# Four graph layers on one core: the softmax division moved behind the value products, leaky relu moved into a ScalarE pass, and the hardware loop written out

## The reference

```python
# layer 0: 8 heads of 16
scores = einsum('bhid,bhjd->bhij', q, k) / sqrt(16) + adj[:, None] * W_e
attn   = softmax(where(adj != 0, scores, -inf), axis=-1)
out    = einsum('bhij,bhjd->bhid', attn, v)      # heads joined, then @ W_o.T
# layer 3: 4 heads of 32
e    = leaky_relu(e_i[..., :, None] + e_j[..., None, :], 0.2)
attn = softmax(where(adj > 0, e, -9e15), axis=-1)
out  = einsum('bhnm,bhmd->bhnd', attn, h)        # heads joined
```

## Time and profile before

| | |
|---|---|
| Median of three timed runs | 2156.44 us (2151.73 to 2159.11) |
| Span of the profiled execution | 2151.3 us; its own time outside the span isn't recorded |
| TensorE matmuls busy | 1993.5 us, 93% of the span |
| VectorE busy | 1669.4 us, 78% |
| ScalarE busy | 1344.1 us, 62% |
| GpSimd busy | 733.6 us, 34% |
| Mean granted TensorE clock | 0.986 of full speed |

### The profile page before, as it was taken

The page is one execution under the profiler, slowest core; times in us unless marked ns, Lnnn a source line. Parts: engine busy times, 40 slices in busy tenths (PEclk is TensorE's granted clock), DMA queues, the critical chain, the costliest instruction groups (busy, mean ns, idle before and its releaser), DMA issues. The chain is left out here.

```text
span 2151.3 us, 43160 instructions
## 1 busy us (share of the span) xinstructions
PE 1993.5 (93%) x13642; PEld 1550.2 (72%) x13642; DVE 1669.4 (78%) x4088; ACT 1344.1 (62%) x4769; POOL 733.6 (34%) x925
## 2 busy tenths in 40 slices
PE   5999999999999999999999999999999999999965
PEld 4777877777777777776777877777776777877643
DVE  4577888878878788787888878778787887888764
ACT  3556667666657667566666656666566666667645
POOL 2233343332343233343333343223343333343220
PEclk9999999999999999999999999999999999999986
DMA  2000000000000000000000000000000000000000
GB/s 84 16 21 21 26 26 21 26 21 12 26 27 21 22 11 26 27 26 22 21 11 26 26 27 21 22 11 26 27 26 22 21 11 27 26 26 6 11 6 10
DMA packets 24296, 47.68 MB, mean 22 GB/s; under 512 B 3283, under 2 KB 3284, under 8 KB 23892
## 3 DMA queue, kind: packets, MB, share of 16 engines
q1 hardware_dynamic: 24020, 44.33, 6.4%
HBM read 35.93 MB, written 8.39 MB: 21 GB/s over the span
## 5 line engine op out<-in xcount | busy, mean ns | idle before, releaser
L759 ACT ACTIVATE e<-sc,nm 128x128 f32<-128x128 f32 x1024 | 399.9, 409 | 65.0 <-DVE nm L995 64.9
L766 ACT ACTIVATE pT<-T 128x512 f32<-128x512 f32 x256 | 158.0, 617 | 299.9 <-PE T L462 299.7
L510 PE MATMUL O<-pT,vpad 128*32 128x128 f32 x2048 | 271.6, 276 | 20.7 <-ACT pT L766 20.7
L992 DVE SCALAR_TENSOR_TENSOR sc<-an,rowb,S 128x512 f32<-128x512 f32 x256 | 189.7, 741 | 124.6 <-PE S L490 78.0
L490 PEld LDWEIGHTS S<-kh,qT 128*128 128x128 f32 x2048 | 268.9, 191 | 9.4
L510 PEld LDWEIGHTS O<-pT,vpad 128*32 128x32 f32 x2048 | 202.9, 109 | 99.3 <-issue 47.2
L490 PE MATMUL S<-kh,qT 128*128 128x128 f32 x2048 | 269.9, 275 | 0.0
L421 POOL TENSOR_SCALAR zplus<-tz 128x512 f32<-128x512 f32 x32 | 28.6, 895 | 596.7 <-issue 571.1
L1003 DVE TENSOR_TENSOR p<-e,rec 128x512 f32<-128x512 f32 x256 | 210.4, 822 | 8.8
L759 ACT ACTIVATION_READ_ACCUMULATOR e<-sc,nm 128x1 f32 x1024 | 213.6, 209 | 0.0
L844 ACT ACTIVATE e<-l,nm 128x128 f32<-128x128 f32 x512 | 201.4, 421 | 7.8 <-DVE nm L1139 7.8
(11 more groups left out here) (191 smaller groups left out, 4465.0 us busy)
## 6 DMA issues: line engine op xcount, KB each, us to landing
xt<-in_x_t SPq DMA_DIRECT2D x32, 256.0 KB, 2.7
an<-in_adj_n SPq DMA_DIRECT2D x32, 256.0 KB, 3.1
xn<-in_x_n SPq DMA_DIRECT2D x32, 256.0 KB, 3.7
at<-in_adj_t SPq DMA_DIRECT2D x32, 256.0 KB, 2.7
out_x<-xo SPq DMA_DIRECT2D x32, 256.0 KB, 2.1
wm<-in_mats SPq DMA_DIRECT2D x1, 1472.0 KB, 6.4
wm<-in_mats SPq DMA_DIRECT2D x1, 832.0 KB, 4.5
att<-in_att SPq DMA_DIRECT2D x8, 0.1 KB
```

Source lines behind the costliest of these rows:

```text
L510: last = mm(O[r, b * N:(b + 1) * N], vpad[:, c:c + 32], g(pT0[:, h % 2, :], b), start=(h % 2 == 0 and b == 0), stop=(h % 2 == 1), skip_gro ...
L759: last = fn(g(e0[:, h % 2, :], b), g(sc0[:, h % 2, :], b), ACT.Exp, bias=nm0[:, h % 2, b:b + 1], accum_out=sum0[:, h % 2, b:b + 1])
L766: fn(pT0[:, h % 2, :], T[:, :], ACT.Copy).then_inc(q["pT_ready"], 1)
L992: v.scalar_tensor_tensor(out=sc0[:, h % 2, :], in0=an[p][:, :], scalar=we[:, h:h + 1], in1=S[h % 2][:, :], op0=ALU.mult, op1=ALU.add).then ...
```

## The change

There are three edits.

1. **The division moves.** TensorE now transposes the undivided exponentials `e0` and `e3`. The sums of all heads are kept. In layer 0, VectorE takes one reciprocal of 128x32 sums (`norm`, slot 8), GpSimd spreads it to 128x512 (`spread_sums`), TensorE transposes that into `T` (`sums_T`, slot 11, four transpositions), ScalarE copies it to `recT` (slot 11, in place of the copy of `O`), and VectorE's `out_heads` (slot 10) multiplies `O` by `recT` into `oT`. `project_out` comes after this. In layer 3, `layer3_end` takes one reciprocal of 128x16 sums and multiplies the transposed result by it, ahead of the addition of `x3`.
2. **Leaky relu moves.** ScalarE's pass that adds e_i uses the function Prelu with slope 0.2 and writes `l3` directly. VectorE's max pass and `z3` are gone.
3. **The loop is written out.** All 36 steps are straight code on every engine, and so are the DMA queue's.

```diff
 def steps(eng, step):
-    for t in range(6):
-        step(t // 2, t % 2, phases_of(t))
-    with eng.Fori(3, GROUPS // 2 - 1) as k:
-        step(k, 0, [True] * 6)
-        step(k, 1, [True] * 6)
-    for t in range(GROUPS - 2, GROUPS + 4):
+    for t in range(GROUPS + 4):
         step(t // 2, t % 2, phases_of(t))
...
-            with sp.Fori(2, GROUPS // 2 - 1) as k:
+            for k in range(2, GROUPS // 2 - 1):
...
+            def spread_sums(s):                      # GpSimd, after zx of the step
+                pool.wait_ge(q["rec_done"], s + 1)
+                wait(pool, q["recT_ps"], s)
+                pool.tensor_copy(recx[:, :, :, :], rec0[:, :, :].unsqueeze(3).broadcast_to([128, GB, H0, D0]))\
+                    .then_inc(q["recx_done"], 1)
...
 def probs_T(s, h):                                    # TensorE
-    pe.wait_ge(q["p_ready"], 8 * s + h + 1)
+    pe.wait_ge(q["exp_done"], 8 * s + h + 1)
...
-    transpose4(T, p0[:, h % 2, :]).then_inc(q["tr_ps"], 1)
+    transpose4(T, e0[:, h % 2, :]).then_inc(q["tr_ps"], 1)
...
+            def sums_T(s):
+                pe.wait_ge(q["recx_done"], s + 1)
+                pe.wait_ge(q["pT_ready"], 8 * s + 8)
+                for b in range(GB):
+                    last = nc.tensor.transpose(g(T, b), recx[:, b, :, :].rearrange("p h d -> p (h d)"), ident[:, :])
+                last.then_inc(q["recT_ps"], 1)
...
                     if l0 and i == H0 + 3:
+                        sums_T(t)
                         project_out(t)
...
-                            act.wait_ge(q["pv_ps"], 8 * t + 8)
-                            wait(act, q["wo_ps"], t)
-                            fn(oT[:, :], O[:, :], ACT.Copy).then_inc(q["oT_ready"], 1)
+                            act.wait_ge(q["recT_ps"], t + 1)
+                            wait(act, q["oT_ready"], t)
+                            fn(recT[:, :], T[:, :], ACT.Copy).then_inc(q["recT_ready"], 1)
...
 # ScalarE, layer 3: the exponential of head h, and the bias pass of head h
-                    wait(act, q["p3_ready"], H3 * u + h - 1)
+                    wait(act, q["tr3_ps"], H3 * u + h - 1)
...
-                    wait(act, q["l3_done"], H3 * u + h - 1)
+                    wait(act, q["exp3_done"], H3 * u + h - 1)
                     for b in range(GB):
-                        last = fn(g(z3[:, h % 2, :], b), g(L[:, h % 2, :], b), ACT.Identity,
-                                  bias=h3[:, b, N + h:N + h + 1])
-                    last.then_inc(q["z3_ready"], 1)
+                        last = fn(g(l3[:, h % 2, :], b), g(L[:, h % 2, :], b), ACT.Prelu,
+                                  bias=h3[:, b, N + h:N + h + 1], alpha=SLOPE)
+                    last.then_inc(q["l3_done"], 1)
...
+            def norm(s):                             # VectorE, slot 8
+                dve.wait_ge(q["exp_done"], 8 * s + 8)
+                wait(dve, q["recx_done"], s)
+                v.reciprocal(rec0[:, :, :], sum0[:, :, :]).then_inc(q["rec_done"], 1)
+
+            def out_heads(s):                        # VectorE, slot 10, ahead of masks(t + 1)
+                dve.wait_ge(q["recT_ready"], s + 1)
+                dve.wait_ge(q["pv_ps"], 8 * s + 8)
+                wait(dve, q["wo_ps"], s)
+                v.tensor_tensor(oT[:, :], O[:, :], recT[:, :], ALU.mult).then_inc(q["oT_ready"], 1)
...
 def layer3_end(u, p, k):
+                dve.wait_ge(q["exp3_done"], H3 * u + H3)
+                v.reciprocal(rec3[:, :, :], sum3[p][:, :, :]).then_inc(q["rec3_done"], 1)
+                dve.wait_ge(q["rec3_done"], u + 1)
                 dve.wait_ge(q["o3n_ps"], u + 1)
...
+                v.tensor_tensor(r3[:, :].rearrange("p (c d) -> p c d", d=D3),
+                                L[:, 0, :].rearrange("p (c d) -> p c d", d=D3),
+                                rec3[:, :, :].rearrange("p b h -> p (b h)").unsqueeze(2)
+                                .broadcast_to([128, GB * H3, D3]), ALU.mult).then_inc(q["n3_done"], 1)
+                dve.wait_ge(q["n3_done"], u + 1)
                 dve.wait_ge(ln_out[2], u + 1)
-                v.tensor_tensor(r3[:, :], L[:, 0, :], x3[p][:, :], ALU.add).then_inc(q["r3_done"], 1)
+                v.tensor_tensor(r3[:, :], r3[:, :], x3[p][:, :], ALU.add).then_inc(q["r3_done"], 1)
```

More of the change, by code:

```diff
@@ L113, in build @@
         e0 = sb("e0", [128, 2, W])
-        sum0 = sb("sum0", [128, 2, GB])
-        rec0 = sb("rec0", [128, 2, GB])
-        p0 = sb("p0", [128, 2, W])
+        sum0 = sb("sum0", [128, GB, H0])
+        rec0 = sb("rec0", [128, GB, H0])
+        recx = sb("recx", [128, GB, H0, D0])
+        recT = sb("recT", [128, W])
         pT0 = sb("pT0", [128, 2, W])
@@ L167, in build @@
         e3 = sb("e3", [128, 2, W])
-        sum3 = sb("sum3", [128, 2, GB])
-        rec3 = sb("rec3", [128, 2, GB])
-        p3 = sb("p3", [128, 2, W])
+        sum3 = [sb(f"sum3{p}", [128, GB, H3]) for p in range(2)]
+        rec3 = sb("rec3", [128, GB, H3])
         pT3 = sb("pT3", [128, 2, W])
@@ L424, in step @@
                     pool.tensor_tensor(zx[:, :], zplus[:, :], x1T[:, :], ALU.mult).then_inc(q["zx_done"], 1)
+                if l0:
+                    spread_sums(t)
                 if ahead:
@@ L613, in layer2 @@
                     pe.wait_ge(q["x2T_ready"], u + 1)
-                    wait(pe, q["r3_done"], u - 1)
+                    wait(pe, q["n3_done"], u - 1)
                     for b in range(GB):
@@ L756, in exps @@
                 act.wait_ge(q["nm_ready"], 8 * s + h + 1)
-                wait(act, q["p_ready"], 8 * s + h - 1)
+                wait(act, q["tr_ps"], 8 * s + h - 1)
+                if h == 0:
+                    wait(act, q["rec_done"], s)
                 for b in range(GB):
                     last = fn(g(e0[:, h % 2, :], b), g(sc0[:, h % 2, :], b), ACT.Exp, bias=nm0[:, h % 2, b:b + 1],
-                              accum_out=sum0[:, h % 2, b:b + 1])
+                              accum_out=sum0[:, b, h:h + 1])
                 last.then_inc(q["exp_done"], 1)
@@ L841, in layer3 @@
                     act.wait_ge(q["nm3_ready"], H3 * u + h + 1)
-                    wait(act, q["p3_ready"], H3 * u + h - 1)
+                    wait(act, q["tr3_ps"], H3 * u + h - 1)
+                    if h == 0:
+                        wait(act, q["rec3_done"], u - 1)
                     for b in range(GB):
                         last = fn(g(e3[:, h % 2, :], b), g(l3[:, h % 2, :], b), ACT.Exp,
-                                  bias=nm3[:, h % 2, b:b + 1], accum_out=sum3[:, h % 2, b:b + 1])
+                                  bias=nm3[:, h % 2, b:b + 1], accum_out=sum3[p][:, b, h:h + 1])
                     last.then_inc(q["exp3_done"], 1)
@@ L1121, in layer3 @@
             def layer3(u, i):
[L1122 to L1129, removed]
                 if 5 <= i < 5 + H3:
                     h = i - 5
[L1133 to L1137, removed]
                     dve.wait_ge(q["l3_done"], H3 * u + h + 1)
@@ L1165, in step @@
                         layer2(t - 2, i, p)
-                    if l0 and i in (H0 - 1, H0):
-                        norm(t, i - 1)
                     if l3:
                         layer3(t - 3, i)
-                    if l0 and 0 <= i - 1 < H0 - 2:
-                        norm(t, i - 1)
+                    if l0 and i == H0:
+                        norm(t)
+                    if l0 and i == H0 + 2:
+                        out_heads(t)
                     if l1 and i == 4:
```

34 lines of the change are left out of this document (13 added, 21 removed).

## The result

The changed kernel takes 2251.05 us (median of four runs, 2248.93 to 2251.21) against 2155.53 us for the kernel before: 1.044 times as long, 95% interval 1.0422 to 1.0457, 95.5 us slower. The prediction had the sign and most of the mechanism, but put the time at 2195 us and the end of its range at 2219, so the measured time lies outside.

A forecast was written before the change was run, and what follows sets the result against it. TensorE, in order and filling 61.12 of 62.62 us, was taken as the bound. Span 2151.3 - 49.6 + 66 + 25 + 2 + 0 - 4 gave 2190.7, hence 2195 us measured; range 2163 to 2219.

The forecast's parts named there:

- The jumps: Loop written out: eleven jumps back and their VectorE issue waits go, 4.5 us each, -49.6 us.
- The join: Slot 11: project_out waits behind sums_T, recT and out_heads while TensorE idles; about 2.05 us a step, +66 us.
- GpSimd's spreading: GpSimd's spreading of layer 0's reciprocals ends well ahead of sums_T, so it costs nothing.
- Prelu: ScalarE's bias pass with Prelu costs the same 385 ns as before, so 0; upper end +16 us.
- The gap ahead of `ll`: VectorE finishes ll late, so TensorE waits 0.9 us ahead of the product using it, in 28 steps, +25 us.
- TensorE's transposition of `yT` just doesn't wait: Behind out_heads, yT ends 1.63 us after project_out's start; TensorE transposes it at 1.98 us, without waiting.
- The tail: Steps 32 to 35: max pass and a product go, a multiplication comes; 1.3 us for each of three groups, -4 us.
- only the join shows: Rival: VectorE's lateness is absorbed because ll has more slack than read; 2168 us, chance 0.17.
- faster: Rival: TensorE's two old gaps, at 454.20 and 470.00, disappear as ScalarE gets inputs earlier; 2137 us, chance 0.07.

The follow-up runs named there:

- straight code: The kernel before with its loop written out and nothing else changed; 2105.45 us, ratio 0.9768 to the kernel before.
- Prelu alone: Kernel before, loop written out, two ScalarE copies moved to VectorE, both divisions as before, Prelu replacing VectorE's max pass; 2058.27 us, ratio 0.9550 to the kernel before.
- the two copies: Head 4's transposed exponentials and layer 3's head 1 copied by VectorE instead of ScalarE; on the kernel before with its loop written out, 2068.95 us.
- layer 3's part: Kernel before with loop written out, plus layer 3's division behind its value products and Prelu, layer 0 as before; 2132.19 us.
- the early transpositions of the sums: Changed kernel with sums_T and ScalarE's copy of it moved to slot 10, ahead of layer 3's head 2; 2125.59 us.
- three passes before `ll`: Kernel before with loop written out, plus three unused VectorE reductions ahead of msg; 2169.46 us, ratio 1.0066 to the kernel before.
- two passes before `ll`: Kernel before with loop written out, plus two unused VectorE reductions ahead of msg; 2126.26 us, ratio 0.9864 to the kernel before.

## Why the prediction was wrong

The prediction's sum starts from the span of 2151.3 us; the span after is 2247.2.

- **The jumps**, -49.6 us: right, 48.9 measured alone.
- **The join**, 2.05 us a step: right, 2.01 measured (the prediction's own terms add up to 2.02).
- **GpSimd's spreading** at nothing: right; it took 0.61 us and TensorE never waited for it.
- **Prelu** at the price of the old pass, without a table load: right, these rows of the changed kernel stand against the earlier trace rows:

```profile
L867 ACT ACTIVATE l<-L,h 128x128 f32<-128x128 f32 x512 | 142.0, 376 | 96.0 <-issue 76.6 <-PE L L665 16.5
...
L750 ACT ACT_TABLE_LOAD x1 | 1.3, 1283 | 23.3 <-PE S L471 23.3
```

- **The gap ahead of `ll`**, 0.9 us: right in its place and in what makes it, 1.02 us as idle time and 1.09 us a step as time. Its size is near by luck. Counted from project_out, `ll` starts 1.82 us later than in straight code, not 1.1: front_end 1.14 us late instead of 0.58, and `xo` took 2.84 us instead of 2.48. But TensorE itself is 0.50 us late there, and the slack of 0.29 us was read rightly.
- **"TensorE's transposition of `yT` just doesn't wait"**: wrong. It waits 0.23 us, and from start to start this place costs 0.50 us a step, some 13 us in the full steps, for which the sum had nothing. `yT` was priced at 0.69 us and took 1.41, beside GpSimd's `kh`. In straight code `yT` runs ahead of project_out and `kh` 1.4 us after its start; now `yT` stands behind the join, and `kh` starts 0.3 us after it, because ScalarE copies the keys while TensorE waits. By the Trainium skill, "GPSIMD Engine Reference", section "1. Specifications", GpSimd shares its SBUF interfaces with VectorE, and VectorE instructions with two SBUF inputs contend; the row agrees.
- **The tail**, -4 us: wrong; from the last front_end to the end it is 126.2 us after and 125.7 before. Prelu alone, on straight code with the two copies, gives 3.5 us there. With layer 3's part alone the tail is 126.7 us against 125.9 in straight code, so its division seems to give Prelu's gain back; by which wait wasn't examined.
- **The step that failed** is the one that turned gaps into time, "a new gap of 0.9 us ... +25 us": it counted a gap at its length and took TensorE's clock as full. No term of the sum held the half clock, and neither did an end of the range. The runs show 18 steps longer by 1.62 us, 29 of the 56 us that the forecast missed, with 18 fewer when the gap goes and 15 new ones when such a gap is made by itself. The rows had a warning: the step with a jump has a clock of 0.97, and its own gap ahead of `ll` is the 1.04 us shown above. The late `yT` is another 13 us of the miss, the `ll` term at 1.10 instead of 0.9 us a step 5, and the tail 4.

In numbers, from straight code alone (span 2104.4) to the changed kernel (2247.2) it is 142.8 us: 27 steps at 3.61 us are 97.5 (the prediction had 2.95, or 80); the half clock in them is 29; up to the fourth front_end it is 12.4 (10 forecast, the clock falls in three of these steps too); the last step ahead of the tail is 2.6; single longer steps are 0.8; the tail is +0.3.

The rival "only the join shows" was wrong about the slack, "faster" about ScalarE: the two old gaps are 0.56 and 0.91 us after, as before. Moving work from ScalarE closed them, and the early transpositions of the sums filled part of the second (0.33 us left).

## What to carry to other kernels

An engine that is busy 97% of each step and takes its work in order gained nothing here from another engine's relief; look for what stands directly ahead of its gaps. A chain across three engines in the middle of its list cost its whole latency where it stood, and almost nothing one slot earlier, where other work was at hand. And price a gap of TensorE of about a microsecond at more than its length, at the least as the upper end: here a wait of 1.0 us cost 1.1, plus 1.6 in two steps of three.

## What the runs showed of the hardware

- TensorE's clock went to 1.2 GHz behind a gap ahead of the product with `ll`, by the length of the gap in full steps: 1.22 to 1.58 us, 15 of 27 (three passes before `ll`); 1.01 to 1.35 us, 18 of 27 (changed kernel); 1.04 to 1.06 us, 3 of 11 (kernel before, steps with a jump); 0.88, 1.01 and 1.02 us, all three (layer 3's part). With 0.80 and 0.88 us in two steps (two passes before `ll`), and with 0.76 us or less in the full steps of every kernel, it never did.
- The half clock began 0.8 to 2.3 us after the gap's end and lasted 3.4 us in all these steps. A gap of 1.41 us in the join, by itself, brought none in full steps. Steps of one kernel with the same work and the same gap differ, so more than the work around the gap decides; these runs don't tell what.
- A VectorE pass over two SBUF inputs took 1.29 to 1.63 us beside GpSimd, against 0.69 to 0.73 us without (`yT`, `lr`, `ll`); `lr` took 0.98 us where only its start met a GpSimd instruction.
- A jump back in this program costs 4.4 us (48.9 us for eleven), though the code it jumps to has run before. This counts all that it brings in its step: the wait for `ll` in all eleven, and half clock in three.
